# A twelve-stage model kernel: two chunks of the following attention's normalisation carried out inside two ternary feed-forward blocks

## What is computed

```
def layernorm(x):                      # per token, over the 128 features
    return (x - mean(x)) / sqrt(var(x) + 1e-05)

# ternary feed-forward (L1_ffn, L3_ffn), 128 -> 512 -> 512 -> 512 -> 128
z = layernorm(x)
h = silu((z @ w1.T) * s1) * ((z @ w2.T) * s2)
h = gelu((h @ h1.T) * t1)
h = gelu((h @ h2.T) * t2)
x = x + 0.5 * ((h @ w3.T) * s3)

# attention (L1_attn: rotary attention of 16 heads; L3_attn: a gated recurrence)
z = layernorm(x)
q, k, v, ... = projections of z
x = x + attention(q, k, v, ...) @ wo
```

## Time and profile before

| | us |
|---|---|
| median of 3 runs | 2543.09 |
| lowest and highest run | 2533.59, 2546.54 |
| the profiled execution, its own time | 2534.73 |
| its span, first to last instruction | 2532.9 |
| mean granted clock of PE, share of full speed | 0.932 |
| busy in the span: PE | 2204.3 |
| DVE | 1530.0 |
| ACT | 1191.1 |
| POOL | 357.0 |

### The profile page before, as it was taken

How to read it: one execution, slowest core, us unless ns; L and a number is a source line. 1 busy time by engine, 2 the same in 40 slices (tenths; PEclk the granted TensorE clock), 3 DMA queues, 4 the chain that set the end, 5 groups by cost and what they waited for, 6 DMA issues and landing times. The chain is left out here.

```text
span 2532.9 us, 42863 instructions
## 1 busy us (share of the span) xinstructions
PE 2204.3 (87%) x17077; PEld 1204.8 (48%) x17077; DVE 1530.0 (60%) x2850; ACT 1191.1 (47%) x2086; POOL 357.0 (14%) x552
## 2 busy tenths in 40 slices
PE   5988987987998988997999999899569679985699
PEld 3665664664665664452222222345347553442345
DVE  7986985558977975018787877310865683038600
ACT  4764772445756763212677777421334433134221
POOL 4322331114313320002000000000120100000000
PEclk9999998998999999997899999999876789999799
DMA  3000000010000000002101000000001100000000
GB/s 135 4 6 3 4 6 8 2 49 1 6 6 1 5 7 26 0 1 70 30 21 29 23 27 11 10 1 0 5 5 25 50 1 9 0 1 0 1 0 17
DMA packets 29863, 38.19 MB, mean 15 GB/s; under 512 B 16898, under 2 KB 21250, under 8 KB 28898
## 3 DMA queue, kind: packets, MB, share of 16 engines
q1 hardware_dynamic: 29522, 34.50, 4.4%
q0 software_dynamic: 144, 0.96, 0.2%
HBM read 27.88 MB, written 4.46 MB: 13 GB/s over the span
## 5 line engine op out<-in xcount | busy, mean ns | idle before, releaser
L2220 DVE TENSOR_REDUCE fa_top<-psum 128x1 f32<-128x1024 f32 x256 | 304.9, 1220 | 74.1 <-PE psum L2163 73.2
L2209 ACT ACTIVATE fa_prob<-psum 128x512 f32<-128x512 f32 x512 | 278.5, 596 | 141.8 <-PE psum L2176 140.8
L533 DVE TENSOR_TENSOR scaled<-psum,area_b 128x512 f32<-128x512 f32 x16 | 11.1, 692 | 456.6 <-PE psum L502 456.6
L492 PE MATMUL psum<-hidden_b,area_b 128*128 128x512 f32 x512 | 221.7, 592 | 0.0
L492 PE MATMUL psum<-hidden_a,area_b 128*128 128x512 f32 x512 | 220.4, 592 | 0.0
L2163 PE MATMUL psum<-fa_stack_k,fa_stack_q 72*128 72x512 bf16 x512 | 203.1, 406 | 6.7 <-DVE fa_top L2220 2.9
L2176 PE MATMUL psum<-fa_stack_q,fa_stack_k 74*128 74x512 bf16 x512 | 198.2, 391 | 10.1 <-ACT fa_prob L2209 4.4
L743 POOL TENSOR_TENSOR turn_a<-turn_a,turn_b 128x1024 f32<-128x1024 f32 x64 | 151.1, 2361 | 287.4 <-DVE turn_b L961 287.4
L760 PE MATMUL psum<-area_a,zt 128*128 128x512 f32 x256 | 135.8, 655 | 24.3 <-ACT k_t L892 14.3
L2176 PEld LDWEIGHTS psum<-fa_stack_q,fa_stack_k 74*128 74x128 bf16 x512 | 48.9, 97 | 224.9 <-ACT fa_prob L2209 197.5
L492 PEld LDWEIGHTS psum<-hidden_a,area_b 128*128 128x128 f32 x512 | 97.3, 190 | 122.5 <-issue 122.5
(11 more groups left out here) (360 smaller groups left out, 4285.6 us busy)
## 6 DMA issues: line engine op xcount, KB each, us to landing
area_b<-in_L_ffn SPq DMA_DIRECT2D x2, 2888.0 KB, 9.3
fa_stack_q<-fa_parts_dram SPq DMA_DIRECT2D x144, 32.0 KB
fa_stack_k<-fa_parts_dram SPq DMA_DIRECT2D x144, 32.0 KB
fa_parts_dram<-fa_prob SPq DMA_DIRECT2D x12, 256.0 KB, 2.6
area_a<-in_L_ffn SPq DMA_DIRECT2D x1, 2482.0 KB, 17.9
moved_halves<-y SPq DMA_DIRECT2D x16, 127.0 KB
area_b<-in_L_attn SPq DMA_DIRECT2D x1, 1880.5 KB, 19.5
area_a<-in_L_attn SPq DMA_DIRECT2D x1, 1538.0 KB, 6.7
```

Source lines behind the costliest of these rows:

```text
L492: last = nc.tensor.matmul(psum[:, 4 + n % 2, :], w(name)[:, k * TF_HID + m * P:k * TF_HID + (m + 1) * P], source[:, c, k, :], start=(k == ...
L2209: nc.scalar.activation(prob[:, (2 * s + j) % RING, half * CHUNK:(half + 1) * CHUNK], psum[:, 4 + n % 2, :], ACT.Exp, scale=float(D) ** -0. ...
L2220: nc.vector.tensor_reduce(top[:, g % 2, j, t:t + 1], psum[:, 2 * j:2 * j + 2, :].rearrange("p a n -> p (a n)"), AX.X, ALU.max, negate=True ...
```

## The change

`ChunkNorm` takes two numbers more. With `behind=CHUNKS` a second object, `following`, uses the same semaphores one stage ahead: its events count from where this stage's own normalisation ends. With `begun=2` the object in the attention stage leaves out all five steps for chunks 0 and 1, since they are done. In the feed-forward stages before `l1_attn` and before `l3_attn` (a new entry `ternary_ffn_and_next_chunks` in `STAGES`), DVE computes statistics and `y` of chunk 0 right after adding chunk 0 to `x`, and the same for chunk 1; POOL takes the roots; PE turns chunk 0 into bank 0 between hidden product 2 and down product 1, and chunk 1 into bank 1 between hidden product 3 and down product 2; ACT copies each into `zt` after the gelus of chunk 2 and of chunk 3. The other two ternary stages keep their instructions.

```diff
+NEXT_CHUNKS = 2
...
-    def __init__(self, core, source, out, eps, names=NAMES):
+    def __init__(self, core, source, out, eps, names=NAMES, begun=0, behind=0):
         self.core, self.source, self.out, self.eps = core, source, out, eps
+        self.begun, self.behind = begun, behind
...
     def dve_stats(self, dve, c):
+        if c < self.begun:
+            return
...
-        dve.wait_ge(*self.counted.at(c + 1))
+        dve.wait_ge(*self.counted.at(self.behind + c + 1))
...
     def pe_turn(self, pe, c, bank):
+        if c < self.begun:
+            return
         core, nc = self.core, self.core.nc
-        pe.wait_ge(*self.normed.at(c + 1))
+        pe.wait_ge(*self.normed.at(self.behind + c + 1))
...
-def ternary_ffn(core, area, four_bit=False, ending=False):
+def ternary_ffn(core, area, four_bit=False, ending=False, ahead=False):
...
     norm = ChunkNorm(core, x, core.y, 1e-5)
+    following = ChunkNorm(core, x, core.y, 1e-5, behind=CHUNKS)
+    early = NEXT_CHUNKS if ahead else 0
...
                 for c in range(CHUNKS):
                     norm.pool_root(pool, c)
+                for c in range(early):
+                    following.pool_root(pool, c)
...
                 for c in range(1, CHUNKS):
                     pe_hidden(pe, 1, c)
+                    if 0 <= c - 2 < early:
+                        following.pe_turn(pe, c - 2, psum[:, c - 2, :])
                     pe_down(pe, c - 1)
                 pe_down(pe, CHUNKS - 1)
...
                         act_gelu(act, step, c)
+                        if step and 0 <= c - 2 < early:
+                            following.act_take(act, c - 2, psum[:, c - 2, :])
...
                 for c in range(CHUNKS):
                     dve_add(dve, c)
+                    if c < early:
+                        dve.wait_ge(*added.at(c + 1))
+                        following.dve_stats(dve, c)
+                        following.dve_normalise(dve, c)
...
+def ternary_ffn_and_next_chunks(core, area):
+    ternary_ffn(core, area, ahead=True)
...
-    norm = ChunkNorm(core, x, y, 1e-5)
+    norm = ChunkNorm(core, x, y, 1e-5, begun=NEXT_CHUNKS)
...
-          ("L1_ffn", ternary_ffn, 1), ("L1_attn", l1_attn, 0), ("L1_ffn", ternary_ffn_and_four_bit_weights, 1),
+          ("L1_ffn", ternary_ffn_and_next_chunks, 1), ("L1_attn", l1_attn, 0), ("L1_ffn", ternary_ffn_and_four_bit_weights, 1),
...
-          ("L3_ffn", ternary_ffn, 1), ("L3_attn", l3_attn, 0), ("L3_ffn", last_ternary_ffn, 1)]
+          ("L3_ffn", ternary_ffn_and_next_chunks, 1), ("L3_attn", l3_attn, 0), ("L3_ffn", last_ternary_ffn, 1)]
```

More of the change, by code:

```diff
@@ L304, in dve_stats @@
         last.then_inc(self.merged.handle, 1)
-        dve.wait_ge(*self.merged.at(c + 1))
+        dve.wait_ge(*self.merged.at(self.behind + c + 1))
         nc.vector.tensor_scalar(core.spread[:, self.span(c)], core.moments[:, self.span(c), 1], self.eps, None,
@@ L309, in pool_root @@
     def pool_root(self, pool, c):
+        if c < self.begun:
+            return
         core, nc = self.core, self.core.nc
-        pool.wait_ge(*self.spread_ready.at(c + 1))
+        pool.wait_ge(*self.spread_ready.at(self.behind + c + 1))
         nc.gpsimd.tensor_tensor(core.rstd[:, self.span(c)], core.spread[:, self.span(c)], core.minus_half[:, self.span(c)],
@@ L315, in dve_normalise @@
     def dve_normalise(self, dve, c):
+        if c < self.begun:
+            return
         core, nc = self.core, self.core.nc
-        dve.wait_ge(*self.rstd_ready.at(c + 1))
+        dve.wait_ge(*self.rstd_ready.at(self.behind + c + 1))
         for i in self.tiles(c):
@@ L323, in pe_turn @@
     def pe_turn(self, pe, c, bank):
+        if c < self.begun:
+            return
         core, nc = self.core, self.core.nc
-        pe.wait_ge(*self.normed.at(c + 1))
+        pe.wait_ge(*self.normed.at(self.behind + c + 1))
         if c >= 2:
-            pe.wait_ge(*self.taken.at(c - 1))
+            pe.wait_ge(*self.taken.at(self.behind + c - 1))
         for j, i in enumerate(self.tiles(c)):
@@ L332, in act_take @@
     def act_take(self, act, c, bank):
+        if c < self.begun:
+            return
         core, nc = self.core, self.core.nc
-        act.wait_ge(*self.turned.at(c + 1))
+        act.wait_ge(*self.turned.at(self.behind + c + 1))
         nc.scalar.copy(core.zt[:, c * CHUNK:(c + 1) * CHUNK], bank).then_inc(self.taken.handle, 1)
```

## The result

The changed kernel takes 2526.04 us, the median of 7 runs (2522.62 to 2530.88); the kernel before, in runs beside it and the three of above, 2535.86, the median of 7. That is 9.8 us or 0.4% less by the medians. The ratio of the runs is 0.9956, with a 95% interval of 0.9942 to 0.9971: clear of noise, and under the 0.5% that the prediction drew as its line. Two later series of the same kernel gave 0.9943 (0.9924 to 0.9963) and 0.9952 (0.9935 to 0.9968).

A forecast was written before the change was run, and what follows sets the result against it. PE was taken to bound the feed-forward stages, and a chain of DVE, POOL, DVE, PE, ACT, PE the attention heads. Gains of 7.3 + 4.5 less 1.8 made 10.0 us, 2543.09 to 2533.1 us, range 2522 to 2543.

The forecast's parts named there:

- the side of 0.5%: Whole kernel: a change within 0.5%, 12.7 us, had chance 0.66; faster than that 0.30, slower 0.04.
- The cover in the feed-forward stage: Feed-forward stages: added DVE work, at most 3.9 us a chunk, hides in 15.89 us of idle; DVE, POOL, ACT cost nothing.
- The transposes: Feed-forward stages: PE pays 0.44 us a chunk for four transposes, 1.8 us of cost in all.
- The head of l1_attn: Start of l1_attn: PE starts at once, DVE's first projection read comes 7.3 us sooner, and the shift is handed on whole.
- projections at half clock: Start of l1_attn: a sign of being wrong; the gain there would be 6.3 us in place of 7.3.
- The normalisation of chunk 2 beside POOL's clearing: Head of l1_attn: could take 1.95 us in place of 1.1, costing 0.8; nothing was taken for it.
- PE's wait ahead of the loop: l1_attn before its loop: the ones fill still ends a wait near 3 us; a longer wait would mean wrong.
- The head of l3_attn: Start of l3_attn: earlier keys and values bring the recurrence forward by 4.5 us, bounds 3.0 to 7.1.
- I put the rise near 2265.4: Head of l3_attn: PE's clock rises from half to full near 2265.4, used for the 4.5 us gain.
- the upper bound: Head of l3_attn: 7.1 us gained if PE has full clock throughout.
- the slower rival: Entry into l1_attn's loop: clock stays half longer, 2.2 us a step; ten more steps give 2555 us; chance 0.05.

The follow-up runs named there:

- e1: Changed kernel with only the passage into l1_attn changed, the one into l3_attn as before: 2530.13 us, ratio 0.9969 to the kernel before.
- e2: Changed kernel with only the passage into l3_attn changed, the one into l1_attn as before: 2532.25 us, ratio 0.9981 to the kernel before.
- e7: The changed kernel again, nothing altered, for a second profile: 2524.21 us, 12.8 us under the kernel before by the medians.
- e12: The changed kernel again, nothing altered, for a third profile: 2524.63 us, ratio 0.9952 to the kernel before.
- e10: Changed kernel plus three unused 512-column matmuls on PE ahead of the turn of chunk 2 in l3_attn; profile only: recurrence at 24.57 us.
- e3: Changed kernel with each chunk's four feed-forward transposes made twice, the second time into unread banks; profile only: L1_ffn and L3_ffn 165.0 us each.
- e5: Changed kernel with transposes and copies of chunks 0 and 1 put back at the attention heads: 2526.26 us, ratio 0.9959 to the kernel before.
- e8: Changed kernel plus three unused 512-column matmuls on PE ahead of its wait for the ones fill at l1_attn's loop: ratio 0.9961 to the kernel before.
- e4: Changed kernel with ready units, keys and values put ahead of waiting transposes in l1_attn and l3_attn: ratio 0.9957 to the kernel before.
- e9: Changed kernel with the fill with ones first in SP's queue in l1_attn; profile only: loop entry at 30.77 us.
- e11: Against the changed kernel: transposes and copies back at the heads, ones fill first on SP, work reordered at both heads: 2518.39 us, ratio 0.9927 to the kernel before.

## Why the prediction was right

The direction, the size (10.0 forecast, 9.8 measured) and the side of 0.5% came out. The mechanism held at both heads: e1 and e2 gave each passage's gain by itself, and their sum. That 10.0 and 9.8 lie so close is luck in part: the profiles give 13.0 at the heads where 11.8 was forecast, and 2.9 us of loss in the loop and in the last stage where none was. The absolute figure, 2533.1, was 7 us high, since it was taken off a median of three runs, 2543.09, that four more runs brought to 2535.86; the profiled execution's own figure, 2524.7, was nearer to the 2526.04 measured. By terms:

- **The cover in the feed-forward stage** held. The new work on DVE ended 3.7 us after it began (1100.17 to 1103.90), where 3.9 was allowed, PE never waited for `y` there, and ACT's copy hid.
- **The transposes**: 0.44 us a chunk forecast, 0.43 and 0.44 seen; the stages grew by 0.7 and 0.9 us, 1.6 in all where 1.8 was forecast.
- **The head of l1_attn**: first read 7.3 us sooner forecast, 7.4 measured; handed on to the loop's first matmul as 7.4. PE did start with DVE. Its clock was full throughout the first units in the first profile only; in e7 and e12 it fell 0.7 us in. The prediction named projections at half clock as a sign of being wrong and priced them at 1 us; they cost 0.35 us at the first read and at most 0.2 at the entry. The normalisation of chunk 2 beside POOL's clearing took 1.19 us in place of 1.11, not 1.95. PE's wait ahead of the loop was 3.19 us where it had been 2.89, and 3.76 in e7.
- **The head of l3_attn**: 4.5 forecast, 5.6 measured. The mechanism and the path were right; the term was under-sized because the step "I put the rise near 2265.4" was late. It carried over from before that the clock rises 4.6 us after the first of these products. The rise came at 2264.5 on the new axis, which is 2263.4 on the old one and 2.6 us after the first product, so the last of the four records of chunk 1's keys and values and the transposes of chunk 3 went at full clock. The two together took 3.43 us (2261.92 to 2265.35) where the prediction had 4.3 (2260.82 to 2265.15). The recurrence starts 21.45 us behind the stage's first transposes, where 22.5 was forecast. e10 showed that full clock throughout would have given 7.2, the 7.1 of the upper bound.
- **Not forecast as a term**: the loop took 2.3 us more in the three profiles. This is the slower rival's mechanism, at one step where that rival needed five to eat the gain. The first value products start 34.8 us behind the entry in both kernels; then one more step went at half clock. The timeline of the changed kernel, against the earlier trace rows:

```profile
1208.31 1.94 PE L2221 MATMUL psum<-fa_prob,fa_pair_v 128*32 128x512 f32 x8
...
1213.71 1.94 PE L2221 MATMUL psum<-fa_prob,fa_pair_v 128*32 128x512 f32 x8
...
1218.11 1.06 PE L2221 MATMUL psum<-fa_prob,fa_pair_v 128*32 128x512 f32 x8
```

Two steps took 5.40 and 4.40 us where before they took 3.98 and 3.10: 2.7 us, a little over the 2.2 that a step at half clock was said to cost. e1 and e10 have the same instructions in l1_attn as the changed kernel and had 437.2 and 437.5 us there, as before, while e3 and all three profiles of the changed kernel had 439.2 to 439.7. So the instructions of the stage do not fix it. The long loop stands in four of the six profiles with the changed kernel's instructions there, and in none of the three with those of before (437.0 to 437.1); whether the change makes it likelier is not settled by so few.

The last stage, too, was 0.6 us longer in the three profiles after (165.6 to 165.7 against 165.0). In the window that begins 8 us behind its first DVE instruction the granted clock is 0.72 before (2375.87) and 0.50 after (2371.44): it rises about 1 us later. e2, e3, e5 and e8 had the long form (165.4 to 165.7), e4, e9, e10 and e11 the short one (164.9) and e1 165.2, though e9 has the changed kernel's own instructions in both of its last two stages; so this is not fixed by the instructions either.

The terms as the profiles have them make 8.4 us, the three series 11.2, 14.5 and 12.2 by their ratios of 0.9956, 0.9943 and 0.9952. Their intervals begin at 7.4, 9.4 and 8.1 us, so the terms fall 1 us short of the second. The first of the stages alone ran from 419.1 to 423.4 us over the fourteen profiles, and L2_attn from 140.0 to 144.0, so I take the rest for chance in stages that the change does not touch; that is argued, not shown.

## What to carry to other kernels

Where a stage opens with a chain through one slow queue and the stage before is bound by another engine, the head of that chain can be run in the earlier stage for the price of the engine that bounds it; here 16 transposes, 1.6 us, bought 13. Only the steps at the head of the chain, DVE's and POOL's, need to move: the version with the transposes left at the head was as fast. Look afterwards for what is second: a DMA fill at the end of a serial queue held the next 2.8 us. The wait for it stood in the rows of before, as 2.89 us, but what the fill itself was worth showed only when it was moved.

## What the runs showed of the hardware

- At the head of l3_attn a wait of PE of 2.93 us was followed by half clock until 3.5 us after its end; with three useless matmuls in it the clock stayed full, and the next 4.3 us of work took 2.65 (e10). A second execution of the same program (e7) fell to half before the wait, so where in a burst the clock falls is not given by the program alone.
- At the head of l1_attn half clock in the first units (e7, e12) made the entry at most 0.2 us later, since PE then waits 3.2 to 3.7 us for DVE.
- PE starts behind a barrier within 0.1 us of DVE, 2.15 us after its own last product (1139.90 for both in l1_attn, 2256.14 and 2256.25 in l3_attn).
- A fill of 64 KB with ones, issued behind nine DMAs of 32 KB each, held PE until 5.1 us after the ninth had been issued; with the fill moved to the head of the queue PE went on 1.8 us after the ninth (e9).
- A stage that is not touched (L2_attn) took 140.0 to 144.0 us from run to run with the same instructions in it, so the difference of two profiled spans says little about a change of 0.4%; the stages' heads, equal within 0.4 us wherever one kernel was profiled again, tell it better.
